# Layer 0 in halves of two batches: sixteen rounds of four heads in one program

## The reference

```python
# layer 0: H = 16 heads of K = 128, F = 1024
def _cross_attention(q_in, kv_in, ...):
    qh = (q_in @ wq + bq).reshape(b, q_len, H, K)
    kh = (kv_in @ wk + bk).reshape(b, t, H, K)
    vh = (kv_in @ wv + bv).reshape(b, t, H, K)
    kh = concatenate([kh, broadcast(bias_k)], axis=1)      # a 257th token
    vh = concatenate([vh, broadcast(bias_v)], axis=1)
    weights = softmax(einsum('bqhk,bthk->bhqt', qh, kh) / sqrt(K))
    return einsum('bhqt,bthk->bqhk', weights, vh).reshape(b, q_len, H * K) @ wo + bo

h = layer_norm(x);  x = x + cross_attention(h, ctx, ...1)
h = layer_norm(x);  x = x + cross_attention(h, ctx, ...2)
h = layer_norm(x);  x = x + (gelu(h @ w_fc1 + b_fc1) @ w_fc2 + b_fc2)
# layer 1 (a recurrence over tokens), layer 2 and layer 3 (attentions with small heads) follow
```

## Time and profile before

| | us |
|---|---|
| median of 3 runs | 1403.58 (1402.42 to 1405.81) |
| the profiled execution | 1399.94 |
| its span, first to last instruction | 1398.2 |
| PE busy | 1202.8 (86%) |
| DVE, ACT, POOL busy | 895.1, 634.6, 515.8 |
| first scores of attention 1 and 2 (S0 of round 0) | 51.6, 409.8 |
| a steady round | 38.9 |
| last round of an attention | 36.0 |
| last product of layer 0 | 797.2 |
| first instruction of layer 1's mixing | 814.6 |

### The profile page before, as it was taken

One profiled execution on the slowest core, in us unless ns is written; L12 is line 12 of the kernel. 1 busy time (PEld: TensorE's weight loads), 2 busy tenths in 40 slices (PEclk: granted clock), 3 DMA queues, 4 the chain that ended last, 5 costly groups with the idle time before them and its releaser, 6 DMA issues. The chain is left out here.

```text
span 1398.2 us, 22983 instructions
## 1 busy us (share of the span) xinstructions
PE 1202.8 (86%) x7772; PEld 942.0 (67%) x7772; DVE 895.1 (64%) x2170; ACT 634.6 (45%) x1427; POOL 515.8 (37%) x569
## 2 busy tenths in 40 slices
PE   4899999999689999999977759686576898889994
PEld 3698989998458899999955723332354676666664
DVE  5467667666546676666659243599564665767766
ACT  2356566655226565555534013100322574467770
POOL 2243344443214444344314012245001463167760
PEclk8999999999889999999998869798889899999998
DMA  6010000002000000000100020000002000000000
GB/s 199 16 32 16 30 30 30 30 8 83 0 31 31 31 30 30 23 30 15 61 1 0 9 67 1 0 1 0 0 24 61 1 2 2 0 1 2 2 2 31
DMA packets 32234, 33.56 MB, mean 24 GB/s; under 512 B 3833, under 2 KB 29730, under 8 KB 32162
## 3 DMA queue, kind: packets, MB, share of 16 engines
q1 hardware_dynamic: 31792, 31.73, 7.2%
q10 hardware_dynamic: 370, 0.91, 0.2%
HBM read 27.38 MB, written 1.05 MB: 20 GB/s over the span
## 5 line engine op out<-in xcount | busy, mean ns | idle before, releaser
L489 POOL TENSOR_TENSOR a_prob<-a_prob,a_inv_total 128x512 f32<-128x512 f32 x128 | 133.5, 1043 | 372.5 <-DVE a_inv_total L746 372.5
L1619 DVE CUSTOM_DVE_ANT_0 l_scores<-psum,mask 128x256 f32<-128x256 f32 x384 | 139.8, 421 | 70.8 <-PE psum L1572 70.8
L1629 POOL TENSOR_TENSOR l_scores<-l_scores,l_neg_max 128x512 f32<-128x512 f32 x144 | 147.8, 1041 | 100.7 <-DVE l_neg_max L1619 100.4
L656 ACT ACTIVATE a_prob<-psum,a_neg_max 128x257 f32<-128x257 f32 x256 | 119.3, 473 | 113.2 <-DVE a_neg_max L743 110.7
L1650 ACT ACTIVATE l_prob_T<-psum 128x512 f32<-128x512 f32 x192 | 108.8, 590 | 35.6 <-PE psum L1586 35.6
L1586 PE MATMUL psum<-ident,l_scores 128*128 128x128 f32 x768 | 117.0, 291 | 7.2 <-POOL l_scores L1629 4.1
L1586 PEld LDWEIGHTS psum<-ident,l_scores 128*128 128x128 f32 x768 | 85.5, 146 | 41.8 <-issue 19.2
L749 DVE TENSOR_TENSOR a_probT_lo<-psum,a_probT_hi 128x512 fp32r<-128x512 f32 x128 | 87.8, 686 | 22.2 <-ACT a_probT_hi L660 21.7
L598 PE MATMUL psum<-ident,a_prob 128*128 128x128 f32 x512 | 79.4, 278 | 11.0 <-POOL a_prob_bias L491 11.0
L743 DVE TENSOR_REDUCE a_neg_max<-psum 128x2 f32<-128x514 f32 x128 | 87.2, 681 | 0.0
L399 PE MATMUL psum<-a_k_hi,a_q_hi 128*128 128x258 f32 x256 | 76.9, 300 | 11.4 <-ACT a_prob L656 7.8
(11 more groups left out here) (336 smaller groups left out, 3342.7 us busy)
## 6 DMA issues: line engine op xcount, KB each, us to landing
wq_raw<-in_L_xattn_wq SPq DMA_DIRECT2D x16, 256.0 KB, 2.8
wk_raw<-in_L_xattn_wk SPq DMA_DIRECT2D x16, 256.0 KB, 2.8
wv_raw<-in_L_xattn_wv SPq DMA_DIRECT2D x16, 256.0 KB, 2.8
wo_raw<-in_L_xattn_wo SPq DMA_DIRECT2D x2, 2048.0 KB, 12.3
a_wo_pair<-wo_raw SPq DMA_DIRECT2D x16, 256.0 KB, 2.3
wo_raw<-in_L_xattn_w_fc SPq DMA_DIRECT2D x2, 1024.0 KB, 6.1
x_rows<-in_x SPq DMA_DIRECT2D x1, 1024.0 KB, 5.9
ctx_rows<-in_ctx SPq DMA_DIRECT2D x2, 512.0 KB, 9.6
```

The lines of the kernel that those rows point to most:

```text
L489: pool.tensor_tensor(prob[:, u % 4, :, 0:S], prob[:, u % 4, :, 0:S], rtot[:, u % 4, :].unsqueeze(2).to_broadcast([P, 2, S]), ALU.mult)
L656: act.activation(prob[:, m % 4, q, 0:S + 1], s_bank(m)[:, q, 0:S + 1], ACT.Exp, bias=negm[:, m % 4, q:q + 1], accum_out=tot[:, m % 4, q:q ...
L1619: e = dve.tensor_tensor_reduce(sc[:, i % SC, q, :], s_bank(i)[:, q * S:(q + 1) * S], masks[:, b * NM + q % NM, :], 1.0, BIG, ALU.add, ALU. ...
L1629: pool.tensor_tensor(sc[:, i % SC, :, :], sc[:, i % SC, :, :], m[:, i % SC, :].unsqueeze(2).to_broadcast([P, 2, S]), ALU.subtract).then_in ...
```

## The change

The five stages of layer 0 become one stage, `stage_layer0`, one block with one program for each engine. The order is: attention 1 on batches 0 and 1, attention 1 on batches 2 and 3, attention 2 on the first half, on the second half. Each of these is four rounds of four heads, so there are again sixteen rounds with eight units (four heads x two batches). All are written out; there is no loop.

- An O piece now sums over four heads (24 products), and there are two of them in a round instead of four of 12. A V piece is one token tile with 512 columns (four heads) instead of two tiles with 256.
- Each weight is loaded and cut twice, once for each half of the batches: 512 KB for each of q, k, v, o in a round. POOL cuts them in halves of 128x512 between the normalisations (`cut_half`).
- Layer norms become pieces: X (statistics), Y (scaling), L (transpose, scale, cut), placed in rounds 1 and 2 of each four for the half that rests. C transposes ctx. P transposes the 257th token's probabilities, B makes the four bias products of the round's heads (only on the first half of an attention).
- The MLP's first product on half 0 (F0 to F7) stands in round 15 in place of Q and K; the rest (G is the second product) follows behind round 15.
- The start loads ctx and x by halves and makes K0 to K3 ahead of the layer norm.
- The normed x goes into ctx's rows, so half of ctx is loaded again in layer 1. Layer 1's weights are loaded into layer 0's weight tiles while layer 0 ends.

```diff
+def layer0_orders():
+    base = ("S0 S1 O0 S2 O1 V0 T0 V1 S3 V2 T1 S4 V3 Q0 T2 S5 Q1 K0 T3 S6 K1 A0 T4 A1 "
+            "S7 T5 Q2 Q3 T6 K2 T7 K3 A2 A3").split()
+    last = ("S0 S1 O0 S2 O1 V0 T0 V1 S3 V2 T1 S4 V3 T2 S5 T3 S6 A0 T4 A1 "
+            "S7 F0 F1 T5 F2 F3 T6 F4 F5 T7 F6 F7 A2 A3").split()
...
+    out = {-1: "X0 X1 C0 C1 Y0 Y1 K0 K1 K2 K3 L0 L1 Q0 Q1 Q2 Q3".split()}
+    for i in range(LOOPS):
+        order = base if i < LOOPS - 1 else last
+        if i == 0:
+            order = [s for s in order if s[0] != 'O']
+            order = put(order, 'S1', 'C0', 'C1')
+        elif i % NQ == 0:
+            order = put(order, 'S0', 'P0')
+        if i // NQ % 2 == 0:
+            order = put(order, 'V3', 'B0')
+        if i % NQ == 1:
+            order = put(order, 'V1', 'X0')
+            order = put(order, 'V3', 'X1')
+            order = put(order, 'T3', 'Y0')
+            order = put(order, 'T4', 'Y1')
+        if i % NQ == 2:
+            order = put(order, 'V1', 'L0')
+            order = put(order, 'V2', 'L1')
+        out[i] = order
+    out[LOOPS] = "P0 O0 O1 X0 X1 Y0 Y1 G0 G1 L0 L1 F0 F1 F2 F3 F4 F5 F6 F7 G2 G3".split()
...
 # SP
+                rows(chip.ctx, 'ctx_2048', 0, ld_ctx[0])
+                weights('k', 0)
+                rows(chip.x, 'x', 0, ld_x[0])
+                weights('q', 0)
+                weights('v', 0)
+                weights('o', 0)
+                rows(chip.ctx, 'ctx_2048', 1, ld_ctx[1])
+                rows(chip.x, 'x', 1, ld_x[1])
+                for j in range(1, LOOPS + 1):
+                    for n in 'qkvo':
+                        weights(n, j)
...
 # POOL, a round
+                    norm(0)
+                    norm(1)
+                    if i:
+                        pool.wait_ge(acc_full, USE[i, 'O1'] + 1)
+                    cut_half('o', i, 0)
                     norm(2)
+                    cut_half('o', i, 1)
+                    norm(3)
+                    pool.wait_ge(acc_full, USE[i - 1, 'K3'] + 1)
+                    cut_half('k', i + 1, 0)
+                    if i % NQ == 1:
+                        rstd_of(event_of(i))
+                    norm(4)
+                    cut_half('k', i + 1, 1)
+                    norm(5)
+                    if i % NQ == 2:
+                        h_low(event_of(i))
+                    pool.wait_ge(acc_full, USE[i, 'V3'] + 1)
+                    cut_half('v', i + 1, 0)
+                    norm(6)
+                    cut_half('v', i + 1, 1)
+                    norm(7)
...
 # PE
+                            t = half_of(i) * HT + m
+                            for c in range(NC):
+                                mm = three(acc(n), ctx_hi[:, c, t * P:(t + 1) * P], ctx_lo[:, c, t * P:(t + 1) * P],
+                                           whi['v'][:, c, :], wlo['v'][:, c, :], c == 0, c == NC - 1)
...
+                            for h in range(QUAD):
+                                mm = pe.matmul(acc(n)[0:H0, 0:D], dvm[:, att_of(i), head(i, h), :], raw['o'][:, h, :], start=h == 0, stop=h == QUAD - 1)
...
 # DVE, ahead of all pieces
+                dve.memset(pb_T[0:32, :], 0.0)
+                dve.memset(pb_T[32:33, :], 1.0)
...
 # build
+            m, load = layer1_memory(chip, l01, d, raw)
+            stage_layer0(chip, d, raw, load)
...
+                    run_layernorm(chip, ln_l1(1)(st), context_again)
```

More of the change, by code:

```diff
@@ L86, in tiles_of @@
     return dram.rearrange("b (u p) d -> p (b u) d", p=P)
[L89 to L167, removed]
@@ L322, in stage_cross_attention, with put @@
-def stage_cross_attention(chip, a, raw, weights, h_hi, h_lo, ctx_hi, ctx_lo, make_ln, prefetch):
+QUAD = 4
+NQ = H0 // QUAD
+HB = B // 2
+HT = HALF // P
+LOOPS = 4 * NQ
+U = QUAD * HB
+KW = S + 2
+def layer0_orders():
[3 more added lines that the diff above has]
+            "S7 F0 F1 T5 F2 F3 T6 F4 F5 T7 F6 F7 A2 A3").split()
+    def put(order, behind, *new):
+        at = order.index(behind) + 1
+        return order[:at] + list(new) + order[at:]
+    out = {-1: "X0 X1 C0 C1 Y0 Y1 K0 K1 K2 K3 L0 L1 Q0 Q1 Q2 Q3".split()}
[18 more added lines that the diff above has]
+    out[LOOPS] = "P0 O0 O1 X0 X1 Y0 Y1 G0 G1 L0 L1 F0 F1 F2 F3 F4 F5 F6 F7 G2 G3".split()
+    return out
@@ L463, in _ @@
+                for j in range(1, LOOPS + 1):
+                    for n in 'qkvo':
+                        weights(n, j)
+                for n in 'qkvo':
+                    sp.wait_ge(split[n], LOOPS + 1)
                 prefetch(sp)
@@ new lines, in cut @@
+                def cut(src, hi, lo, ends=None):
+                    pool.tensor_tensor(hi, src, one[:, 0:1].unsqueeze(2).to_broadcast([P] + list(src.shape[1:])) if len(src.shape) == 3
+                                       else one[:, 0:1].to_broadcast([P] + list(src.shape[1:])), ALU.mult).then_inc(rounded, 1)
+                    cuts[0] += 1
+                    pool.wait_ge(rounded, cuts[0])
+                    lo_ = pool.tensor_tensor(lo, src, hi.bitcast(F32), ALU.subtract)
+                    if ends is not None:
+                        lo_.then_inc(ends, 1)
@@ new lines, in cut_half @@
+                def cut_half(n, j, c):
+                    if c == 0:
+                        pool.wait_ge(ld[n], 16 * (j + 1))
+                    part = (lambda t: t[:, 2 * c:2 * c + 2, :]) if n == 'o' else (lambda t: t[:, c, :])
+                    hi, lo = (whi[n], wlo[n])
+                    if n == 'o' and j == LOOPS:
+                        pool.wait_ge(acc_full, USE[LOOPS - 1, 'A3'] + 1)
+                        hi, lo = w2b_hi, w2b_lo
+                    cut(part(raw[n]), part(hi), part(lo), split[n] if c else None)
@@ new lines, in add_b2, with norm @@
+                def add_b2(e):
+                    pool.wait_ge(ln_norm, HT * (e + 1))
+                    r = ROWS.index('L0_xattn_b_fc2')
+                    t = slice(e % 2 * HT, (e % 2 + 1) * HT)
+                    pool.tensor_tensor(chip.x[:, t, :], chip.x[:, t, :], chip.rows[:, r:r + 1, :].to_broadcast([P, HT, D]), ALU.add).then_inc(b2_ok, 1)
+                rstd_of(0)
+                cut_half('v', 0, 0)
+                h_low(0)
+                cut_half('v', 0, 1)
+                for i in range(LOOPS):
+                    def norm(m):
+                        h, b = m // HB, m % HB
+                        pool.wait_ge(s_sum, i * U + m + 1)
+                        pool.tensor_tensor(prob[:, m % 4, :, 0:S], prob[:, m % 4, :, 0:S],
+                                           rtot[:, m % 4, :].unsqueeze(2).to_broadcast([P, 2, S]), ALU.mult)
+                        hh = head(i, h)
+                        pool.tensor_tensor(pb[:, i // NQ % 2, 2 * b:2 * b + 2, hh:hh + 1], prob[:, m % 4, :, S:S + 1], rtot[:, m % 4, :].unsqueeze(2),
+                                           ALU.mult).then_inc(s_norm, 1)
@@ L850, in three @@
                     return pe.matmul(out, l_lo, r_hi, start=False, stop=last)
-                for n in range(NU):
-                    f = n // 2
-                    pe.wait_ge(w1_ok, f // 2 + 1)
-                    if n >= 4:
-                        pe.wait_ge(gelu, n - 3)
-                    for c in range(NC):
-                        mm = three(ps[:, n % 4, :], w1_hi[:, c, part(f)], w1_lo[:, c, part(f)], h_hi[:, c, half(n)], h_lo[:, c, half(n)], c == 0, c == NC - 1)
-                    mm.then_inc(full, 1)
@@ L860, in _, with project @@
[L860 to L866 removed]
+                def project(n, w, h, src_hi, src_lo, half):
+                    cols = slice(half * HALF, (half + 1) * HALF)
+                    for c in range(NC):
+                        mm = three(acc(n), whi[w][:, c, h * K0:(h + 1) * K0], wlo[w][:, c, h * K0:(h + 1) * K0],
+                                   src_hi[:, c, cols], src_lo[:, c, cols], c == 0, c == NC - 1)
+                    mm.then_inc(acc_full, 1)
```

925 lines of the change are left out of this document (439 added, 486 removed).

## The result

The kernel after takes 1418.22 us (median of 6 runs, 1417.34 to 1421.16), the kernel before beside it on the same chip 1407.34: a ratio of 1.0082, 95% interval 1.0054 to 1.0110. It is 0.8% slower, where I had forecast 3.3% faster. The profiled execution took 1417.65 us, 17.7 more than that of before. Of the runs further down, one each of the last two versions took 3943 and 4667 us for no cause that the record shows; these two are left out of the medians.

The account below looks back on a forecast made before the run. PE was taken to bound steady rounds, with seams between. 40 + 38.9 + 578.7 + 43 + 54.6 = 755.2 instead of 797.5 (-42.3), and -4.1, gave 1353.5 profiled; 3.6 more made 1357 us, range 1348 to 1366.

Parts of the forecast that it names:

- Part 2: POOL cutting weights twice, 7.0 us more a round: hidden, 0 for steady rounds, bounds 0 and +3.5 us a round.
- Rival (c): Normalisations 3 to 7, each behind a cut: POOL becomes the clock and T waits; 1413 us, chance 0.07.
- POOL idle 14 us a round: Sign in the rounds that the forecast is right: POOL still idle 14 us in each.
- Part 1: Products in steady rounds: only V changes shape, 0.15 us less, so 38.75 us a round.
- Part 4: The start, up to S0 of round 0: 40 us instead of 51.6, bounds 33 and 47.
- Part 5: Round 0: 38.9 us after 38.7, with clearing moved to the start and C0, C1 and B0 added.
- Part 6: Rounds 1 to 14 with the added pieces inside them: 578.7 us together, from 14 x 38.75 = 542.5.
- Parts 7 and 8: Round 15 and the tail behind it: 43 and 54.6 us, 97.6 together.
- Part 7: Round 15 with F0 to F7: 38.75 us plus +4.3 of stalls from table loads, 43; bounds 39 and 47.
- Part 9: Way from layer 0 to layer 1's mixing: loads issued in layer 0's tail, -4.1 us, bounds -5 and 0.
- Rival (a): Start, round 15, tail and layer norms: everything covers, -24 us at most, halfway 1343 us; chance 0.14.

## Why the prediction was wrong

The step that failed is in Part 2. I wrote "I followed POOL's new order through a round", listed when normalisations 2 to 7 end, held them against T2 to T7 and concluded "The cuts are hidden". I had laid only the normalisations against their readers. The cuts themselves have readers too: the halves of wk against K0, of wo against O0, of wv against V0. My own list has normalisation 4 ending at 22 us, and the second half of wk behind it takes 2.3: 24.3, for a K0 that comes at 20 to 21 (20.6 in the round of before that is shown below, whose S0 begins at 167.17). That is 3 to 4 us late, and it stood in my numbers.

The trace of before would have shown it without any estimate. Its round from 168.1, POOL's cut of wk and its fifth normalisation, then K0:

```profile
180.43 1.29 POOL L473 TENSOR_TENSOR a_wk_lo<-wk_raw,a_wk_hi 128x512 fp32r<-128x512 f32 x1
...
187.61 1.04 POOL L489 TENSOR_TENSOR a_prob<-a_prob,a_inv_total 128x512 f32<-128x512 f32 x1 [1.68 <-DVE a_inv_total L746]
...
187.81 0.39 PE L399 MATMUL psum<-ctxT_hi,a_wk_hi 128*128 128x512 f32 x1
```

There the cut is done at 181.72, 6.1 us ahead of K0. Normalisation 4 (187.61, and 0.2 for its bias column) ends at 188.8 and waits for DVE, whatever POOL has to do before it. A cut behind it ends 2.4 us later, at 191.2, 3.4 us after K0 is due; the kernel before with the cut there showed a gap of 3.5.

What it cost, against the version with wk's cuts first, from S0 to S0: round 11, a gap of 2.14 us and no slow stretch, is 2.3 longer (42.6 against 40.3). Round 7, a gap of 4.21 and 3.4 us at the lower clock, is 5.9 longer (44.2 against 38.3): 4.2 and 1.7. Rounds 1 to 14 of the kernel after and of that version:

```profile
80.40:722.50 642.10, 584.14 (x3598) 501.63 (x3598) 379.99 (x700) 327.36 (x807) 352.22 (x405) 0.97 0.15 47
81.20:663.10 581.90, 564.24 (x3599) 488.18 (x3599) 388.07 (x700) 328.83 (x807) 353.69 (x406) 1.00 0.16 52
```

That is 60.2 us more. PE is idle for 58.0 against 17.7, so 40.3 of it is waiting. The other 19.9 is the clock, which is at the lower level twelve times in eleven of these rounds, 3.4 us each (41.0 in all, 1.7 lost each time).

- "I take 0 for steady rounds; bounds 0 and +3.5": measured 60.2 / 14 = 4.3. The bound was half of the 7 us added to POOL, a measure of load. What an in-order queue costs is how late the needed item ends, and that can't be read off the sum of work. The clock wasn't in the bound at all.
- Rival (c), slower at 1413, came nearest in size, but not in its mechanism. It had T waiting since POOL runs out of time. POOL waited for 310.7 us in all for DVE's reciprocals, and with the same load in another order the kernel takes 1357. T's waits for POOL are there, but small: 3.5 us in rounds 1 to 14 of the kernel after. "POOL idle 14 us a round" was no safeguard: it was 20.5 in round 7 of the kernel after and 14.1 with wk's cuts first.
- Part 1 held: 0.16 us a round by V, 0.15 forecast.
- Part 4: 39.0 in the kernel after, 41.7 and 39.3 in the two runs with wk's cuts first, forecast 40. Part 5: 41.1, of which 2.3 is K0's gap; 39.2 and 38.7 in the two runs with wk's cuts first (38.9). Its base of 38.7 was 0.9 too long, since the bound at 90.3 lies behind S0: from S0 to S0 (51.57 to 89.38) the old round 0 took 37.8, and the new one 40.6, then 38.8 and 38.3.
- Part 6: 581.9 and 582.0 without the fault, forecast 578.7. The excess of 3.2 is less than T7's waits for POOL in rounds 2, 6, 10 and 14 (5.5 us); Part 2 had said that h_low uses up the 2 us to spare there, and put it at nothing.
- Parts 7 and 8: 97.3 together, 98.2 with wk's cuts first, 97.6 forecast; the split between them wasn't measured apart. That three table loads lie on the path was one of my grounds for the +4.3 of Part 7. What they cost stays open: two fewer changed nothing in all, and PE waits behind such a load in both orders.
- Part 9: -5.2, forecast -4.1, and the loads are the cause.
- Rival (a) had a slip of its own: half of -24 from 1357 is 1345, not 1343.

So the sum of the other eight parts, 1357 us, is what the kernel takes once the cuts stand in time (1357.80 and 1356.93). That agreement is partly luck. The working gives 1353.5 for a profiled execution, and these took 1359.12 and 1356.5: 3.0 to 5.6 us short, the rounds alone 3.2. What makes it up is the 3.6 us by which the median of before lay above its profiled execution; the new version's medians don't lie above theirs in that way (1.3 below and 0.4 above).

On the SBUF interfaces that, by the Trainium skill (GPSIMD Engine Reference, section 1), POOL shares with DVE, the traces show contention, at POOL's cost. In the version with wk's cuts first the second normalisation of a round, which takes 1.04 us elsewhere, takes 1.94 beside DVE's low part of wq, an instruction with two SBUF inputs:

```profile
295.60 1.21 DVE L714 SCALAR_TENSOR_TENSOR a_wq_lo<-wq_raw,a_wq_hi 128x1024 fp32r<-128x1024 f32 x1
295.77 1.94 POOL L444 TENSOR_TENSOR a_prob<-a_prob,a_inv_total 128x512 f32<-128x512 f32 x1 [0.65 <-DVE a_inv_total L729]
```

It happens in twelve rounds, each time beside that instruction, which takes 1.20 to 1.22 us from round 1 on with or without it. It leaves no mark on PE: round 7 has one of the same 1.94 us and takes 38.6.

## What to carry to other kernels

When items are moved or added in an in-order queue, write for every item the time at which it can end (behind the last thing ahead of it that waits for another engine) and the time at which its first reader comes, and do it for the new items before the old ones; idle time in the engine says nothing about this. The trace of the kernel before has both times: shift the item and read how late it is. If the reader is an engine that bounds the kernel, add to the wait what the lower clock behind a gap costs, here 1.6 us for each slow stretch behind a gap of 3.5 us.

## What the runs showed of the hardware

- A gap of PE in an otherwise full round often brings 3.4 us at the lower clock behind it, in which 512 columns take 0.42 us instead of 0.23. Gaps of up to 1.6 us (the cuts one place earlier) never did in rounds 1 to 14. In the kernel after, gaps of 2.1 us did in rounds 3 and 8 and didn't in round 11; of 3.46 us in the altered kernel before, they did in nine middle rounds and not in three (1, 6 and 13). What tells these apart was not found.
- The price of such a stretch is its length times the share lost: 1.6 us of 3.4 in rounds that differ in nothing else, near the half.
